# The attention loop of a fused block: how many score steps TensorE issues before it turns to side work and values

## The reference, cut to what matters

```
s = einsum('bthd,bshd->bhts', q, k) * scale
logits = 2 * log(abs(s) + 1e-30) + log_G[:, :, :, None] - log_G[:, :, None, :]
m = max(logits, axis=-1)                      # causal
a = exp(logits - m)                           # = (s * decay)^2 / row maximum
num = einsum('bhts,bshd->bthd', a, v);  den = sum(a, axis=-1)
y = num / (den + 1e-6);  y = (y - mean) / sqrt(var + 1e-9) * ln_w
out = y.reshape(B, T, 1024) @ w_proj
```

## Time and profile before

| | |
|---|---|
| median of 3 runs | 1057.96 us (1056.93 to 1059.55) |
| the profiled execution, its own time | 1058.96 us |
| its span, first to last instruction | 1056.9 us |
| mean granted TensorE clock | 0.985 |
| busy: TensorE matmul / VectorE / ScalarE / GpSimd | 94% / 83% / 63% / 57% |

### The profile page before, as it was taken

One profiled execution on the slowest core, in us unless ns is written; L12 is line 12 of the kernel. 1 busy time (PEld: TensorE's weight loads), 2 busy tenths in 40 slices (PEclk: granted clock), 3 DMA queues, 4 the chain that ended last, 5 costly groups with the idle time before them and its releaser, 6 DMA issues.

```text
span 1056.9 us, 23328 instructions
## 1 busy us (share of the span) xinstructions
PE 994.3 (94%) x8871; PEld 684.2 (65%) x8871; DVE 874.1 (83%) x1730; ACT 670.4 (63%) x1077; POOL 606.8 (57%) x593
## 2 busy tenths in 40 slices
PE   4999989999998999999999999999999999999884
PEld 2675565666665767676767676767676676767563
DVE  5678748898989998988998879898888899889972
ACT  1342445766666677777677868676878766776551
POOL 0311538888897565565756374756475666557421
PEclk9999999999999999999999999999999999999896
DMA  9301214443433353543544353545253335445530
GB/s 259 95 2 46 55 52 110 109 98 96 104 101 97 99 147 83 134 98 83 123 123 119 98 136 83 121 107 139 71 129 89 88 98 138 101 91 126 137 106 21
DMA packets 77951, 108.65 MB, mean 103 GB/s; under 512 B 15853, under 2 KB 46445, under 8 KB 77712
## 3 DMA queue, kind: packets, MB, share of 16 engines
q1 hardware_dynamic: 72768, 104.50, 38.8%
q0 software_dynamic: 5072, 2.67, 1.9%
HBM read 31.61 MB, written 11.36 MB: 41 GB/s over the span
## 4 chain that ended last, share of the span: by engine, by line
PE 74%; DVE 11%; POOL 4%; DMA 4%; issue 3%; ACT 2%; SPq 2%; POOLq 0%; DVEq 0%; ACTq 0%
PE PS L713 20%; PE PS L521 19%; PE PS L742 18%; PE PS L516 6%; PE PS L564 2%; PE PS L567 2%; PE PS L574 2%; DVE PS L1304 2%; DMA U<-H_d 2%; POOL U L1407 1%; SPq L461 1%; POOL xe_d L1439 1%; POOL Kt L1410 1%; DVE U L1271 1%; PE PS L537 1%
## 5 line engine op out<-in xcount | busy, mean ns | idle before, releaser
L713 PE MATMUL PS<-Qt,Kt 64*128 64x256 f32 (+1 forms) x2560 | 295.4, 370 | 8.1 <-DVE U L1271 7.1
L713 PEld LDWEIGHTS PS<-Qt,Kt 64*128 64x128 f32 x2560 | 219.6, 187 | 81.4 <-issue 51.7
L742 PE MATMUL PS<-U 128*64 128x256 f32 (+1 forms) x1792 | 191.6, 354 | 11.4 <-ACT U L899 11.4
L888 ACT ACTIVATE U<-PS 128x1024 f32<-128x1024 f32 x192 | 188.2, 1016 | 11.1 <-PE PS L713 8.1
L884 ACT ACTIVATE U<-U 128x768 f32<-128x768 f32 x128 | 107.7, 841 | 113.1 <-DVE U L1271 112.9
L742 PEld LDWEIGHTS PS<-U 128*64 128x64 f32 x1792 | 121.6, 138 | 87.6 <-issue 32.1
L1407 POOL TENSOR_TENSOR U<-U,consts 128x512 f32<-128x512 f32 x96 | 125.1, 1303 | 88.7 <-DMA U<-U 88.7
L1304 DVE SCALAR_TENSOR_TENSOR PS<-U,ES,PS 128x512 f32<-128x512 f32 x192 | 144.8, 754 | 17.7 <-ACT U L888 8.7
L1271 DVE SCALAR_TENSOR_TENSOR U<-PS,U 128x768 f32<-128x768 f32 x128 | 119.5, 953 | 42.6 <-PE PS L713 35.5
L1429 POOL TENSOR_SCALAR_AFFINE_SELECT U<-U 128x256 f32<-128x256 f32 x128 | 70.0, 547 | 105.4 <-ACT U L812 104.8
L1475 POOL TENSOR_TENSOR U<-U,SM 128x1024 f32<-128x1024 f32 x32 | 61.0, 1906 | 77.6 <-DVE SM L1324 77.5
(11 more groups left out here) (163 smaller groups left out, 1542.1 us busy)
## 6 DMA issues: line engine op xcount, KB each, us to landing
G<-U SPq DMA_DIRECT2D x512, 64.0 KB
U<-U SPq DMA_DIRECT2D x192, 128.0 KB, 2.4
U<-H_d SPq DMA_DIRECT2D x32, 512.0 KB
Kt<-Kt SPq DMA_DIRECT2D x32, 256.0 KB, 3.8
U<-in_w SPq DMA_DIRECT2D x21, 256.0 KB
acc<-in_x SPq DMA_DIRECT2D x4, 512.0 KB, 5.6
ye_d<-G SPq DMA_DIRECT2D x4, 512.0 KB, 8.3
U<-ye_d SPq DMA_DIRECT2D x4, 512.0 KB, 5.2
```

Of the source, the lines that this page charges most:

```text
L713: mm = te.matmul(bank[:, 256 * n:256 * n + 256 - lo], Kt[u % 2][(ki + hd) % 2][rows, 128 * j:128 * j + 128], Qt[p % 2][m // 2][rows, 256 * ...
L742: mm = te.matmul(P[4][64 * hd:64 * hd + 64, c + lo:c + 256], vt, A[s % NA][:, o:o + 256 - lo], start=i == 0 and n == 0, stop=i == m and n ...
L888: s.activation(A[n % NA], PS[:, first:first + 1024], ACT.Square, scale=0.125, bias=GUARD).then_inc(a_sq, 1)
```

## The change

TensorE goes in groups of five steps, two groups a pair. A group is: five score steps, the side jobs of ten ticks, then values. The group of steps 0 to 4 is followed by values 0 to 3 *of the same group*, the group of steps 5 to 9 by value 4 and values 5 to 9. There are 8 tiles A in place of 4 (two of them carved out of space that is free in the loop, two from a new SBUF buffer). All five tables of times are new; among other things the scales of steps 0, 1 and 4 stand close together on VectorE, and on ScalarE the squares stand in the order of steps, with the copy "nt" 0 between squares 3 and 4. Each unit still starts with its diagonal step.

```diff
-PAIRS, NA, BATCH, HS = ((0, 1), (2, 3), (6, 7)), 4, 2, 130
+PAIRS, NA, BATCH, HS = ((0, 1), (2, 3), (6, 7)), 8, 5, 130
...
-ACT_AT = [(9.22, "nt", 0), (18.95, "nt", 1), (-1.16, "square", 0), (-0.5, "square", 1), (0.26, "square", 2),
-          (0.64, "square", 3), (5.62, "square", 4), (6.52, "square", 5), (10.9, "square", 6), (10.92, "square", 7),
-          (13.7, "square", 8), (14.72, "square", 9), (-8.44, "decay", 0), (-3.62, "decay", 1), (-1.59, "decay", 2),
+ACT_AT = [(10.56, "nt", 0), (19.82, "nt", 1), (-0.16, "square", 0), (0.67, "square", 1), (1.03, "square", 2),
+          (1.35, "square", 3), (10.63, "square", 4), (10.87, "square", 5), (11.21, "square", 6),
+          (12.01, "square", 7), (12.27, "square", 8), (12.36, "square", 9), (-6.67, "decay", 0), (-2.75, "decay", 1),
...
-DVE_AT = [(27.09, "fold", 0), (28.83, "max", 0), (1.62, "scale", 0), (2.35, "scale", 1), (10.29, "scale", 4),
-          (13.78, "scale", 6), (6.3, "top", 0), (8.43, "top", 2), (12.46, "top", 3), (12.75, "top", 5),
-          (19.39, "top", 7), (19.46, "top", 8), (19.66, "top", 9), (52.68, "wp", 0), (53.61, "wp", 1),
+DVE_AT = [(15.64, "fold", 0), (17.44, "max", 0), (-5.1, "scale", 0), (-4.83, "scale", 1), (-3.29, "scale", 4),
+          (5.63, "scale", 6), (-4.38, "top", 0), (-1.44, "top", 2), (-1.05, "top", 3), (5.68, "top", 5),
+          (7.19, "top", 7), (9.15, "top", 8), (10.91, "top", 9), (38.86, "wp", 0), (44.62, "wp", 1),
...
-        take = carve(5120)
+        take = carve(3072)
+        MORE = [take(1024) for _ in range(2)] + [AX_[:, 1024 * i:1024 * i + 1024] for i in range(NA - 6)]
         SWPk = take(1024)
...
-        A = [take(1024) for _ in range(NA)]
+        A = [take(1024) for _ in range(4)] + MORE
...
                 for job in jobs_of(s):
                     side(job)
-                for n in range(max(s - BATCH, 0), min(s, 320)):
+                first, last = (s, s + 4) if s % 10 == 0 else (s - 1, s + 5)
+                for n in range(first, min(last, 320)):
                     values(n)
```

More of the change, by code:

```diff
@@ L72 @@
[L72 to L75, removed]
+PE_AT = [(26.53, "max", 0), (15.15, "y", 0), (26.46, "y", 1), (40.48, "fin", 0), (45.76, "fin", 1), (43.79, "wp", 0),
[3 rows of a table added]
+ACT_AT = [(10.56, "nt", 0), (19.82, "nt", 1), (-0.16, "square", 0), (0.67, "square", 1), (1.03, "square", 2),
+          (1.35, "square", 3), (10.63, "square", 4), (10.87, "square", 5), (11.21, "square", 6),
+          (12.01, "square", 7), (12.27, "square", 8), (12.36, "square", 9), (-6.67, "decay", 0), (-2.75, "decay", 1),
+          (-2.34, "decay", 2), (3.1, "decay", 3), (15.58, "y", 0), (23.02, "y", 1), (41.91, "fin", 0),
+          (42.16, "fin", 1), (29.2, "ysq", 0), (27.75, "xe", 0), (38.22, "up", 0), (38.5, "up", 1), (44.9, "up", 2),
+          (48.04, "up", 3), (65.56, "down", 0), (-26.4, "k", 0), (-23.19, "k", 1), (-13.86, "q", 0), (-12, "q", 1),
+          (-24.83, "v", 0), (-4.93, "v", 1)]
@@ new lines @@
+DVE_AT = [(15.64, "fold", 0), (17.44, "max", 0), (-5.1, "scale", 0), (-4.83, "scale", 1), (-3.29, "scale", 4),
+          (5.63, "scale", 6), (-4.38, "top", 0), (-1.44, "top", 2), (-1.05, "top", 3), (5.68, "top", 5),
+          (7.19, "top", 7), (9.15, "top", 8), (10.91, "top", 9), (38.86, "wp", 0), (44.62, "wp", 1),
+          (17.92, "sum", 0), (25.4, "var", 0), (28.94, "root", 0), (31.69, "root", 1), (33.11, "root", 2),
+          (42.57, "up", 4), (43.5, "up", 5), (47.8, "up", 6), (48.02, "up", 7), (-27.22, "k", 0), (-26.57, "k", 1),
+          (-16.82, "q", 0), (-16.15, "q", 1)]
@@ L76 @@
+POOL_AT = [(61.29, "combine", 0), (69.62, "combine", 1), (83.77, "combine", 2), (-7.09, "select", 0),
+           (-6.61, "select", 1), (-6.02, "select", 2), (3.17, "select", 3), (-9.87, "vs", 1), (-2.04, "vs", 2),
+           (-1.89, "vs", 3), (22.24, "n1", 0), (36.22, "n2", 0), (-21.07, "k", 0), (-15.47, "k", 1), (-8.17, "q", 0),
+           (-6.67, "q", 1)]
 SCATTER_AT = [5 * c / 2 for c in range(64 - EARLY)]
@@ L78 @@
 SP_FIRST = [("row", 0), ("swapk", 0), ("swapq", 0), ("keys", 0)]
-SP_AT = [(-2.12, "rows", 0), (6.13, "rows", 1), (7.47, "rows", 2), (8.39, "rows", 3), (-28.09, "swapk", 0),
-         (-20.83, "swapq", 0), (-17.52, "keys", 0), (-15.94, "row", 0), (7.46, "weights", 0), (7.8, "weights", 1)]
+SP_AT = [(-9.3, "rows", 0), (-5.94, "rows", 1), (4.27, "rows", 2), (5.57, "rows", 3), (-31.74, "swapk", 0),
+         (-27.94, "swapq", 0), (-20.01, "keys", 0), (-27.08, "row", 0), (-2.77, "weights", 0),
+         (19.53, "weights", 1)]
 LOAD_AT = [20 * EXPERT_PAIRS[-1] + 76 + b for b in range(B)]
@@ L230, in block_program @@
         Qt = [[sb(f"Qt{i}{half}", 512) for half in range(2)] for i in range(2)]
+        AX_ = sb("AX", 1024 * (NA - 6))
         NU = 25920
```

8 lines of the change are left out of this document (removed), and 6 rows, old and new, of the table PE_AT.

## The result

The changed kernel takes **1095.68 us** (median of 4 runs, 1095.06 to 1103.31) against 1058.2 for the kernel before beside it: ratio 1.0367, 95% interval 1.0326 to 1.0408. It is slower, as forecast, but by 37.5 us where I forecast 6, and it lies outside my range (1040 to 1090). One of the eight executions of a later run, `after_rot32`, took 5524 us and is left out of that run's ratio. The profiled execution took 1096.21 us, its span 1094.1; mean granted clock 0.984 (before: 0.985).

What follows compares the result with a forecast made beforehand. TensorE's instruction list was taken as the bound. The sum 1058.96 - 33.6 - 11.4 + 44.2 + 7 - 2.5 = 1062.7 us, 1061.7 at the median, became a forecast of 1064 us, range 1040 to 1090.

Steps and rivals of the forecast that it cites:

- the ladder: TensorE's waits for PSUM banks still being read, in both groups of a pair: 32 x (0.92 + 0.46) = +44.2 us.
- the first group's wait: First transpose after scores 0 to 4 waits for ScalarE's square 2 to free its bank: 0.92 us a pair.
- the second group's: First transpose after scores 5 to 9 waits for square 7: 0.29 us a pair.
- the 0.17 before score 8: In the second group, score 8 waits for its bank until square 5 ends: 0.17 us a pair.
- Fewer changes between kinds: TensorE's switches between kinds of matmul: five groups a pair become two, saving 3 x 32 x 0.35 = 33.6 us.
- The copy's wait: First value step of units 0 and 2 no longer waits for ScalarE's copy of bank 4: -11.4 us.
- The tail: Last pair's first score to its last maximum shrinks from 27.0 to about 24.5 us: -2.5 us.
- the last pair's stall: VectorE's eight final additions stall TensorE by 4.27 us; the prediction left that unchanged.
- VectorE a little late: Scales late by 0.4 us at two places, in 9 even pairs without expert jobs in their first group: +7 us.
- VectorE becomes late at both scales: Rival: VectorE meets each group of scores 0.45 us or more late, 29 us in all, 1093 us; chance 0.3.
- nothing to spare: VectorE's list from scale 0 to scale 6, about 12.9 us, against TensorE's way of 13.9 less 1.10 us.

Runs made afterwards that it cites:

- after_rot32: GpSimd's two rotation products narrowed from 512 to 32 columns in the kernel after: 1055.7 us; the same cut in the kernel before: 1046.1 us.
- the pair with both cuts: VectorE's row maxima and GpSimd's rotation products both narrowed, in the kernel after (1043.7 us) and in the kernel before (1033.9 us).
- max32: VectorE's maxima narrowed from 512 columns to 64 (some to 32), in the kernel after (1064.9 us) and in the kernel before (1045.1 us).
- after_memset: Each GpSimd rotation product replaced by four chained fills of 400 columns, in the kernel after: 1079.32 us.
- one_input: VectorE's small root instructions made to read one tensor and 15 columns instead of two tensors and 16, in the kernel after: 1104.71 us.

## Why the prediction was right, and where it was wrong

*The direction, and the ladder.* Right in mechanism, and close in sum. 32 x (0.92 + 0.29) = 38.7 us was forecast before the first transposes, and SF measured 41.0, in 63 places (two for each pair); with VectorE unloaded, 39.8. The parts cancel in part: the first group's wait was 0.81 us where I had 0.92, the second group's 0.49 where I had 0.29, and the 0.17 before score 8 (5.4 us in all) is not there. For the second group the sum, 0.46 forecast, is right, but the whole of it falls before the transpose.

*Fewer changes between kinds: -33.6.* Right in mechanism, a little large. In the pair with both cuts the waits grew by 40.3 and the time by 9.6, so 30.7 us came back; with rot32 or max32 alone, by the stretch from the first score to the last value, 30.6. In the full kernels it is 27. The clock doesn't explain the missing 3.7 us: over that stretch the mean granted clock is 0.991 after and 0.992 before. Where they are is open.

*The copy's wait: -11.4.* Right: PV is 13.3 before and 0 after.

*The tail: -2.5.* Wrong sign. From the last pair's first score to its last maximum, 27.0 us before and 24.5 in my forecast, it is 32.2. In that stretch lie waits that other rows of the table below count, the last pair's stall above all, which I left as it is. It grew from 4.27 us to 6.88:

```profile
1040.92 3.36 PE L716 MATMUL PS<-Qt,Kt 64*128 64x256 f32 x16 [6.88 <-DVE AX L1275]
```

From the last value step to the end it is 31.2 us, 30.4 before.

***VectorE a little late: +7.* This is the step that failed.** With 5.4 for the ladder's part before score 8 I had 12.4 us of growth in SS; it grew by 28.8, and none of that is the ladder's. FF and FP, where I had nothing, grew by 8.3; among them is the wait for the late fold. I took 0.4 us at two places in nine pairs; in seven of these nine (without the first and the last) scale 0 came 1.84 us late on average. My rival "VectorE becomes late at both scales", 1093 us at 0.3, is nearest to what happened (and my range, which ended at 1090, left out its own figure): SS, FF and FP grew by 37.1 us, 2.6 of them the last pair's stall, so some 34 us of waiting for VectorE, where the rival had 7 + 29 = 36. It took another way than the rival's, though: not through the squares to the first transpose (SF stayed), but straight to the fourth score step, whose bank scale 0 reads, and to "max".

Three things stood behind it. First, I added VectorE's list up from durations of before, which no longer held: 52 us more for the same instructions, because small jobs, the fold and a unit's first maximum came to lie beside GpSimd's products. Second, I wrote "nothing to spare" and then priced the lateness at a sixth of the ladder; with a list of 12.9 us in a way of 12.8, each further microsecond of VectorE goes into TensorE's time. Third, I overlooked what covered lateness before: there scale 0 came 1.00 us late on average in the same seven pairs, and TensorE had values and side jobs to go on with before it needed that bank; in the new order the fourth score step needs it 2.4 us after the first.

The difference between forecast and measurement, against the profiled spans (37.2 measured, 3.7 forecast, so 33.5):

| term | forecast | measured | off by |
|---|---|---|---|
| scores behind banks (SS: ladder 5.4, VectorE 7) | +12.4 | +28.8 | +16.4 |
| transposes behind squares (SF) | +38.7 | +40.7 | +2.0 |
| transposes and products behind the fold (FF, FP) | 0 | +8.3 | +8.3 |
| products behind the expert weights' DMA (PP) | 0 | +4.3 | +4.3 |
| PV, VV, PS and the rest | -11.4 | -18.4 | -7.0 |
| fewer changes, and what the ledger does not place | -33.6 | -26.9 | +6.7 |
| before the first score and behind the last value | -2.5 | +0.4 | +2.9 |

The terms come from one execution of each kernel. That the first row is VectorE's is shown by rot32 and max32 (SS 9.3 and 14.1, of which 6.3 and 6.1 are the last pair's stall); the third row grows by 10 with max32, 4 with rot32 and 1 with both, so it goes with GpSimd's products first; the weights' row (4.2 us in 4 places in the waits above) is seen, not tested.

What stays open: how much of the 24 us between after_memset and after_rot32 GpSimd's shorter chain is worth, the 3.7 us above, and whether a table exists in which five-step groups pay. None that I ran with the full work was faster than the kernel before. Even without VectorE's lateness the change loses 9.7 us: by the pair with both cuts the ladder costs 39, the weights 6 and the scores (the last pair's stall above all) 7, with 2 in smaller rows; the copy gives 13 back and the changes 31.

## What to carry to other kernels

Longer groups of one kind save a fixed price for each change, and take slack out of every queue that reads behind them: count both, by the readers' bursts and not by their busy share. Where a second engine is within a few per cent of the bound, terms don't add: taking 41 us of one wait away gave 1 us, within the noise, while VectorE was late, and 11 when it was not. And before VectorE's list is moved, look at what GpSimd does in its new place, since a duration measured beside idle GpSimd is a different one beside a product.

## What the runs showed of the hardware

- A 128x16 float32 VectorE instruction in SBUF takes 0.17 us, and 1.1 to 1.2 when a 1.28 us GpSimd product runs beside all of it; it ends 30 to 44 ns behind the product. One that met a mask (`select`) and a product behind it took 1.92 us. A 128x15 one with one tensor is held too (mean 412 ns for L1351 of one_input). GpSimd fills of 0.446 us hold the one-tensor instructions (29 of 40 in after_memset over 0.25 us, up to 0.51) and not those with two (1 of 153).
- A VectorE instruction of which one tensor lies in PSUM was not stretched: the running maxima take 216 us in after, in before and in after_rot32.
- The whole effect is large: narrowing GpSimd's products takes 82 us off VectorE's busy time in after and 32 in before, for the same VectorE instructions.
- The stretch around the 6.88 us in which TensorE stood still (1030 to 1045 us) has a granted clock of 0.77, and from 1038 to 1044 us it is 0.50, which is the level of 1.2 GHz: TensorE had stood still since 1034.03 when it fell, and was at work again since 1040.92 when it rose. Most windows of the loop have 1.00 (2.4 GHz), those at 500 and 800 us 0.98; in the one at 500 the clock is 0.57 from 536 to 540, behind the 2.02 us wait shown above.
